# A fused attention and FP4 feed-forward block on one core: VectorE sums three key tiles instead of two, and POOL folds that sum into its own

## The reference

```
x = x + attention(layernorm(x))
x = x + ffn(layernorm(x))

attention: xn = layernorm(x) * gamma + beta ; q, k, v = split(xn @ w_qkv)   (16 heads of 64)
           q, k = rotate(q), rotate(k)
           probs = softmax(q k^T / 8) ; out = (probs v) @ w_out + b_out
ffn:       gate, up, down products on operands rounded blockwise to FP4; silu(gate) * up between
```

## Time and profile before

| | us |
|---|---|
| median of three runs | 1664.45 |
| profiled execution, device time | 1665.25 |
| its span in the profile | 1663.4 |
| PE busy | 1569.4 (94%) |
| POOL busy | 1332.8 (80%) |
| DVE busy | 1178.7 (71%) |
| ACT busy | 721.7 (43%) |

### The profile page before, as it was taken

One profiled execution on the slowest core, in us unless ns is written; L12 is line 12 of the kernel. 1 busy time (PEld: TensorE's weight loads), 2 busy tenths in 40 slices (PEclk: granted clock), 3 DMA queues, 4 the chain that ended last, 5 costly groups with the idle time before them and its releaser, 6 DMA issues.

```text
span 1663.4 us, 25122 instructions
## 1 busy us (share of the span) xinstructions
PE 1569.4 (94%) x9513; PEld 816.1 (49%) x9513; DVE 1178.7 (71%) x1440; ACT 721.7 (43%) x941; POOL 1332.8 (80%) x761
## 2 busy tenths in 40 slices
PE   3899999999999999999999999999999999997666
PEld 1345555554554554555545545555554554554445
DVE  4777776667777777767677777766777777654776
ACT  1244444544444544544444545444444544542222
POOL 4578888778888888988778888898778889865673
PEclk9799999999999999999999999999999999999797
DMA  4111111111111111111111111111111111100000
GB/s 127 43 30 42 46 46 38 46 46 44 42 27 46 46 33 46 46 38 46 46 46 41 30 43 46 33 46 46 38 45 46 45 41 33 28 16 15 13 13 26
DMA packets 69191, 67.06 MB, mean 40 GB/s; under 512 B 26512, under 2 KB 52432, under 8 KB 69072
## 3 DMA queue, kind: packets, MB, share of 16 engines
q1 hardware_dynamic: 69072, 65.46, 15.7%
HBM read 29.25 MB, written 2.62 MB: 19 GB/s over the span
## 4 chain that ended last, share of the span: by engine, by line
PE 82%; DVE 14%; POOL 2%; issue 2%; ACT 0%; DMA 0%; DVEq 0%; POOLq 0%
PE po L1085 28%; PE st L1072 20%; PE mx L1123 10%; PE ms L1108 8%; DVE negmax L821 5%; PE ms L1096 4%; PE ms L1149 4%; PE ms L1140 4%; DVE max_rows L835 3%; PE ms L1131 1%; DVE probs L778 1%; PE mx L1208 1%; DVE amax L772 1%; PE st L1208 1%; POOL psum_keys L367 1%
## 5 line engine op out<-in xcount | busy, mean ns | idle before, releaser
L821 DVE TENSOR_REDUCE negmax<-mx 128x2 f32<-128x1024 f32 x504 | 615.7, 1222 | 358.9 <-PE mx L1123 358.9
L621 ACT ACTIVATE probs<-st 128x1024 f32<-128x1024 f32 x512 | 497.0, 1022 | 487.1 <-PE st L1072 487.1
L367 POOL TENSOR_TENSOR psum_keys<-psum_keys,probs 128x1024 f32<-128x1024 f32 x256 | 608.0, 2375 | 110.6 <-ACT probs L621 90.3
L1085 PE MATMUL po<-probs,v 128*64 128x512 f32 x2048 | 495.7, 605 | 0.0
L1072 PE MATMUL st<-heads 64*128 64x512 f32 x3072 | 419.3, 391 | 0.0
L1072 PEld LDWEIGHTS st<-heads 64*128 64x128 f32 x3072 | 289.7, 185 | 59.3 <-issue 2.4
L1085 PEld LDWEIGHTS po<-probs,v 128*64 128x64 f32 x2048 | 124.3, 136 | 255.8 <-issue 146.9
L1123 PE MATMUL mx<-heads 64*128 64x512 f32 x1008 | 239.5, 471 | 9.6 <-DVE negmax L821 3.6
L367 POOL TENSOR_TENSOR psum_keys<-probs 128x1024 f32<-128x1024 f32 x64 | 152.0, 2375 | 58.5 <-ACT probs L621 58.5
L1123 PEld LDWEIGHTS mx<-heads 64*128 64x128 f32 x1008 | 94.5, 184 | 196.2 <-issue 117.3
L498 POOL TENSOR_TENSOR kq<-kq 128x1024 f32<-128x1024 f32 x64 | 152.1, 2376 | 39.8 <-DMA kq<-sin_part 39.7
(11 more groups left out here) (145 smaller groups left out, 1228.5 us busy)
## 6 DMA issues: line engine op xcount, KB each, us to landing
kq<-sin_part SPq DMA_DIRECT2D x256, 128.0 KB, 2.4
rsum<-recips SPq DMA_DIRECT2D x128, 128.0 KB, 3.0
wqkv<-in_L_attn_w_qkv_dram SPq DMA_DIRECT2D x32, 192.0 KB, 2.8
resid<-in_L_attn_x_dram SPq DMA_DIRECT2D x4, 512.0 KB, 8.5
wout<-in_L_attn_w_out_dram SPq DMA_DIRECT2D x32, 64.0 KB, 2.6
out_dram<-resid SPq DMA_DIRECT2D x8, 256.0 KB, 2.3
sums<-sums_kept SPq DMA_DIRECT2D x64, 4.0 KB
spread<-sums SPq DMA_DIRECT2D x64, 4.0 KB, 1.6
```

What stands on the lines that cost most here:

```text
L367: nc.gpsimd.tensor_tensor(psum_keys[:, c], first, probs[:, (STEPS * P + i) % RING], ALU.add)\
L621: nc.scalar.activation(probs[:, step_n % RING], st[step_n % 2][:, :], ACT.Exp, scale=SCALE)\
L821: nc.vector.tensor_reduce(negmax[:, t // HALF, :, t % HALF, half], banks[:, :], AX.X, ALU.max, negate=True)\
L1085: last = mm(po[HD * a:HD * a + HD, :], v[:, P % 2, KEY_ORDER[jt], HD * a:HD * a + HD], probs[:, step_n % RING, a], start=(jt == 0), stop=( ...
```

## The change

VectorE reduces three tiles instead of two. POOL's first add comes one step later (tiles 3 and 4), and after its last tile it adds `first_sum` into `psum_keys`. So POOL has 5 adds a half as before, now four of tiles and one of VectorE's sum. PE makes the products with ones from `psum_keys` alone, four instead of eight. VectorE's wait before it overwrites `first_sum` is now for POOL's sum of the pair before in place of the S unit.

```diff
-FIRST_KEYS = 2
+FIRST_KEYS = 3
@@ keys_added
-        return (JT - FIRST_KEYS - 1) * (2 * P + c)
+        return (JT - FIRST_KEYS) * (2 * P + c)
@@ add_step (POOL)
             nc.gpsimd.tensor_tensor(psum_keys[:, c], first, probs[:, (STEPS * P + i) % RING], ALU.add)\
               .then_inc(key_sum, 1)
+            if jt == JT - 1:
+                pool.wait_ge(key_sum, keys_added(P, c) + JT - FIRST_KEYS - 1)
+                pool.wait_ge(key_part, 2 * (2 * P + c) + 2)
+                nc.gpsimd.tensor_tensor(psum_keys[:, c], psum_keys[:, c], first_sum[:, c], ALU.add).then_inc(key_sum, 1)
@@ first_keys (DVE)
-                filled(dve, ("S", P - 1, c))
+                dve.wait_ge(key_sum, keys_added(P - 1, c + 1))
@@ softmax_sums (PE)
-            pe.wait_ge(key_part, 2 * (2 * F + c) + 2)
             pe.wait_ge(key_sum, keys_added(F, c + 1))
-            for part in (first_sum, psum_keys):
-                for j in range(4):
-                    a, quarter = j // 2, bass.ts(j % 2, QUARTER)
-                    last = mm(ms[32 * j:32 * j + 32, 0:QUARTER], ones[:, 0:32], part[:, c, a, quarter],
-                              start=part is first_sum, stop=part is psum_keys)
+            for j in range(4):
+                a, quarter = j // 2, bass.ts(j % 2, QUARTER)
+                last = mm(ms[32 * j:32 * j + 32, 0:QUARTER], ones[:, 0:32], psum_keys[:, c, a, quarter],
+                          start=True, stop=True)
```

## The result

| | before | after |
|---|---|---|
| median us (4 runs each) | 1664.42 | 1675.73 (1674.01 to 1676.59) |
| ratio of the runs | | 1.007, 95% interval 1.0052 to 1.0087 |
| profiled execution, its span | 1665.25, 1663.4 | 1676.59, 1674.8 |
| pair 16 | 45.40 | 45.69 |

The forecast was 1662.8 with a range up to 1672. The kernel is slower by 0.7%: the interval of the ratio lies wholly above 1.

What follows compares the result with a forecast made beforehand. PE was taken to set the time, with DVE in a few places. Ordinary pairs +2.9, pairs 5, 13, 21 +1.7, pairs 0 and 1 -1.1 and -0.6, pair 31 -1.2: 1.7 us faster, median 1662.8, range 1657 to 1672.

Steps and rivals of the forecast that it cites:

- the price of the reduce: DVE's four reduces a pair, each reading 1536 elements a partition instead of 1024: between 0.50 and 0.62 us more each.
- x = 0.52: Time in us added to each three-tile reduce on DVE, taken from the row at 1408 elements; 1739 to 1755 ns there.
- the end of 0.62: Upper bound in us on a reduce's added time, in proportion to the tiles: 1239 x 1.5 = 1859 ns.
- the same sum by places: An ordinary pair: PE's 0.86 us less DVE losses of 0.08, 0.46 and 0.21, a gain of 0.11; 26 such pairs +2.9.
- 1.67 - 3x: Net gain in us of an ordinary pair, x being the time added to each reduce, for x above 0.45.
- the special pairs: Pairs 5, 13 and 21 gain 1.7 us together; pair 0 loses 1.1 and pair 1 about 0.6.
- the sign of the dear reduce: In the profile after, a pair period above 45.6 us would show the reduce dearer than forecast.
- What PE saves: S units, PE's products with ones: two matmul groups fewer, 0.43 us a unit, 0.86 a pair, 27.5 over 64 units.
- The four places: DVE delays to PE: slot 1 into 2 0.08 us, 3 into 4 0.46, 5 into 6 free, 6 into 7 0.21.
- Pair 31: Last pair: POOL's chain 2.5 us longer, last product 0.43 shorter, a loss of 2.1; with the tail -1.2.
- POOL has cover elsewhere: POOL's new add before the product: 2.4 us of cover left in half 0, more in half 1, so no loss.
- Slower: the reduce costs in proportion to the tiles: Rival, chance 0.19: 0.62 us added in slots 1, 3 and 6, a pair nets -0.19; 7.5 us slower, 1672.

## Why the prediction was wrong

- **The failed step is the price of the reduce.** "No row has three tiles in a group, so I bound it", and "I take x = 0.52". Measured was 0.674, beyond even the end of 0.62. The rows at 1408 and 512 elements that set the slope are maxima over 16 elements side by side; the row at 1024, with its elements apart, had two in a group, and groups of two pay nothing for that. I measured nearness by the count of elements, not by how they lie. Why threes apart are dearer no run shows. The Trainium skill's one cycle an element ("VectorE: DVE Perf Modes", section "The TRN2 errata — SBUF-src ops pay a fixed extra latency per instruction") gives 0.53, which the form side by side keeps to (0.51 to 0.53). For the form of this kernel the measurement decides against it. (At that slope the three rows leave 0.14 to 0.17 us over, not 0.14 to 0.21.)
- **The mechanism stands.** With x = 0.674, the same sum by places gives 1.67 - 3x = -0.35 us a pair, and with the special pairs and the last one some 12.5 us slower, about 1677; measured 1675.7. Pair 16 lost 0.29, and its 45.69 us lie beyond the 45.6 that the prediction named as the sign of the dear reduce. The formula "for x above 0.45, it is 1.67 - 3x" was confirmed at 0.506 (a median ordinary pair of 45.22 us, by the formula 45.26) and at 0.674 (45.70, by the formula 45.76). With both products kept the places give 46.39, measured 46.37.
- *What PE saves*: 0.43 us a unit; 27.5 forecast, 28.3 measured alone, 0.86 a pair in the trace.
- *The four places*: slots 3 and 6 together 0.94 us a pair (0.98 by the formula), slots 1 and 5 together 0.23 (0.23).
- *Pair 31*: forecast 2.5 us in POOL's chain; its wait grew by 2.4 and the pair by 1.5 (29.37 to 30.90), with 0.86 saved in it.
- *POOL has cover elsewhere*: right for five adds a half. It would not have been for six.
- *The rivals*: "Slower: the reduce costs in proportion to the tiles" was the right one in its sign and in its places, and still too cheap. Its reason was wrong too: side by side, three tiles cost 1753 ns and not 1859, so it is not the count of tiles that sets the price. It said that the sum turns at 0.54. With a turning point 0.02 from my value, and no row for the form in question, it deserved more than 0.19, and the range more than its 1672.

## What to carry to other kernels

An engine at 71% busy can be the bound at single points: look for zero idle time behind the instruction that grows, not at its share. When a sum comes out near zero as the difference of two large terms, its error is that of the worst-known price times its count, here 3 per pair. A price is taken from a row with the same access pattern, not only the same count of elements. And work moved to an engine with room on the mean must be checked in the stretches where that engine has other work.

## What the runs showed of the hardware

- A tensor_reduce of float32 over groups of three or more whose elements lie 8 or more apart is dearer than side by side: three 1912 against 1753 ns, four 3619 against 2286, five 4471 against 2820, for 512 results. Groups of two differ by 1% at most (1219 to 1231 against 1220). Threes and fours 2 apart cost as side by side. The cause is not shown.
- Beside POOL's adds, a tensor_tensor with two SBUF inputs on VectorE takes up to 2.8 times as long as alone (3434 to 1225 ns): one that starts beside a POOL instruction ends 1.08 to 1.09 us after it. POOL's own add grows from 2374 to 2483 ns on the mean.
- PE's four column products of 256 float32 columns start 0.22 us apart as a group, so a whole set of eight matmuls costs 0.43 us in line, whatever the mean of one (379 ns) says: without one such set in each of its two units a pair is 0.86 us shorter.
